# GpSimd's convolution multiplies: one operation of 512 columns in place of two of 256

## Reference

```python
qkvz = x @ W_in                                   # 128 -> q, k, v, z of 1024 each
qkv = conv_general_dilated(concat([q, k, v]), conv_w,      # four taps, one filter per channel,
                           padding=[(3, 0)], ...)          # over the tokens of one sequence
q, k, v = split(silu(qkv))
q = l2norm(q) * HD ** -0.5;  k = l2norm(k)        # 16 heads of 64
def step(S, inp):                                 # per token, per head
    S = S * exp(gt)
    S = S + k (v - k S) * beta
    o = q S
y = norm_w * rmsnorm(o) * silu(z);  x = x + y @ W_o
```

## Time and profile before

| | |
|---|---|
| median of 3 runs | 6077.84 us (6057.86 to 6098.86) |
| the profiled execution | 6087.45 us, of which 6085.7 us from the first to the last instruction |
| PE busy | 5156.0 us (85%) |
| DVE busy | 3611.1 us (59%) |
| ACT busy | 2854.3 us (47%) |
| POOL busy | 2789.0 us (46%), 3045 instructions |
| mean granted TensorE clock | 0.930 |

### The profile page before, as it was taken

One profiled execution on the slowest core, in us unless ns is written; L12 is line 12 of the kernel. 1 busy time (PEld: TensorE's weight loads), 2 busy tenths in 40 slices (PEclk: granted clock), 3 DMA queues, 4 the chain that ended last, 5 costly groups with the idle time before them and its releaser, 6 DMA issues. The chain is left out here.

```text
span 6085.7 us, 206341 instructions
## 1 busy us (share of the span) xinstructions
PE 5156.0 (85%) x78381; PEld 3866.5 (64%) x78382; DVE 3611.1 (59%) x6984; ACT 2854.3 (47%) x5746; POOL 2789.0 (46%) x3045
## 2 busy tenths in 40 slices
PE   4899999999999999999999776688887899994496
PEld 3666666666666666666666555566665666663496
DVE  6666666666666666666666664544444666664443
ACT  1555555555555555555555413333332455451175
POOL 5766666666666666666666533400001000005453
PEclk9999999999999999999999988899898999995598
DMA  3000000000000000000000103200000000001124
GB/s 111 20 25 25 24 25 25 23 24 23 25 25 24 25 24 25 24 25 25 24 25 25 39 20 65 66 1 0 0 0 2 1 0 0 0 0 54 36 70 128
DMA packets 126297, 167.29 MB, mean 27 GB/s; under 512 B 33016, under 2 KB 110880, under 8 KB 123052
## 3 DMA queue, kind: packets, MB, share of 16 engines
q1 hardware_dynamic: 94924, 123.07, 6.7%
q0 software_dynamic: 14080, 26.64, 1.3%
q10 hardware_dynamic: 16640, 8.39, 0.7%
HBM read 118.84 MB, written 105.69 MB: 37 GB/s over the span
## 5 line engine op out<-in xcount | busy, mean ns | idle before, releaser
L934 PE MATMUL bank<-wc,shifted 128*128 128x512 f32 (+1 forms) x2344 | 1055.9, 570 | 19.0 <-issue 15.7
L1324 ACT ACTIVATE TT<-bank 128x512 bf16<-128x512 f32 x640 | 374.0, 595 | 540.7 <-PE bank L1060 289.4
L934 PEld LDWEIGHTS bank<-wc,shifted 128*128 128x128 f32 x2344 | 403.6, 194 | 299.3 <-issue 287.0
L1411 POOL TENSOR_TENSOR qa<-qa,qt 128x512 f32<-128x512 f32 x390 | 487.7, 1272 | 34.8 <-POOL qt L1406 34.8
L1406 POOL TENSOR_TENSOR qt<-qp,cq 128x256 f32<-128x256 f32 x780 | 474.6, 639 | 23.2 <-POOL qa L1411 23.2
L1089 PE MATMUL bank<-X,kqe 64*64 64x64 f32 x12480 | 447.1, 221 | 24.7 <-DVE rb L1593 19.6
L1640 DVE TENSOR_TENSOR yb<-bank,masks 128x512 bf16<-128x512 f32 x512 | 352.0, 687 | 185.6 <-PE bank L1041 185.6
L1089 PEld LDWEIGHTS bank<-X,kqe 64*64 64x64 f32 x12480 | 399.7, 134 | 71.1 <-issue 52.5
L1324 ACT ACTIVATE T<-bank 128x512 bf16<-128x512 f32 x512 | 287.1, 595 | 252.4 <-PE bank L1053 250.4
L3280 DVE TENSOR_REDUCE mxp_full<-bank_full 128x2 f32<-128x512 f32 x524 | 325.7, 685 | 108.7 <-PE bank_full L3029 108.7
L1041 PEld LDWEIGHTS bank<-T,mTb 128*128 128x128 bf16 x5120 | 202.7, 97 | 253.1 <-ACT T L1324 81.1
(11 more groups left out here) (547 smaller groups left out, 12974.1 us busy)
## 6 DMA issues: line engine op xcount, KB each, us to landing
sent_l0f<-blank_l0f SPq DMA_DIRECT2D x64, 528.0 KB
sent_l1m<-blank_l1m SPq DMA_DIRECT2D x64, 528.0 KB
xin<-sent_l1m SPq DMA_DIRECT2D x139, 66.0 KB
taken_l1m<-back_l1m SPq DMA_DIRECT2D x16, 512.0 KB, 8.7
xin<-sent_l0f SPq DMA_DIRECT2D x75, 66.0 KB
x_sb<-in_L_attn_x_dram SPq DMA_DIRECT2D x32, 128.0 KB, 2.9
cw_stage<-in_L_attn_conv_w_dram SPq DMA_DIRECT2D x4, 1024.0 KB, 6.5
x_rows<-x_sb ACTq DMA_DIRECT2D x8, 512.0 KB, 11.8
```

Of the source, the lines that this page charges most:

```text
L934: mm = pe.matmul(bk[:, cols], src[:, j, :], w["wc"][:, j, at * 512 + cols.start:at * 512 + cols.stop], start=(j == 0), stop=(j == TAPS - 1 ...
L1324: nc.scalar.activation(dst, bk[:, :].rearrange("p (h a u) -> p h a u", h=8, u=1 << l), ACT.Copy).then_inc(actb.done.sem, 1)
L1411: ins = pool.tensor_tensor(qa[:, H, :], qa[:, H, :], qt[:, H, :], ALU.add)
```

## The change

In `convolve` the loop over the two sequences goes; one multiply of 4 groups x 2 sequences x 64 columns takes their place. The access pattern of its input steps over groups, over sequences (67 columns apart) and over tokens; the tap is broadcast over the last two. The waits, the adds and all else stay as they are. One convolution has 8 multiplies of 512 columns and the same 6 adds.

```diff
                 for n, j in enumerate((TAPS - 1, *range(TAPS - 1))):
                     for half, H in enumerate(halves):
-                        for s in range(NB):
-                            at = s * (LEAD + BS) + j
-                            tap = w["cq"][:, H, j:j + 1].to_broadcast([P, 4, BS])
-                            ins = pool.tensor_tensor((qt if n else qa)[:, H, of(s)], qp[:, H, at:at + BS], tap, ALU.mult)
+                        x = qp[:, H, :].rearrange("p k (s n) -> p k s n", s=NB)[:, :, :, j:j + BS]
+                        tap = w["cq"][:, H, j:j + 1].unsqueeze(3).to_broadcast([P, 4, NB, BS])
+                        ins = pool.tensor_tensor((qt if n else qa)[:, H, :].rearrange("p k (s n) -> p k s n", s=NB), x, tap,
+                                                 ALU.mult)
                         if n and half:
                             chain(b, ins)
```

## The result

The changed kernel takes 6170.79 us (median of 4 runs, 6151.45 to 6182.0) against 6088.35 (4 runs, 6057.86 to 6098.9): ratio 1.014, 95% interval 1.009 to 1.019. The profiled executions are 6149.7 and 6085.7 us from the first to the last instruction.

The account below looks back on a forecast made before the run. PE's program order was taken to bound the delta stage. DVE's delays of 3.56 us a turn over 16 turns, 57.0 us, less 1.2 once, gave +56 us: 6077.84 to 6134 us, range 6090 to 6170.

Parts of the forecast that it names:

- The price of the operation: POOL's new 512-column multiply in the convolution: 1.05 us at the broadcast rate, 0.43 more than the old one.
- The turn-taking, t = 1, 2, 3: DVE's masks and copy wait for whole POOL multiplies at tile start: +1.14, +0.86 and +0.86 us a tile.
- t = 0: First tile of each loop turn: DVE held 1.28 us longer, less PE's slack, leaving +0.70 us.
- slack 0.58: In t = 0, PE's second level_zero group could have started 0.58 us earlier, absorbing that much of DVE's delay.
- What DVE loses PE loses: At level_zero PE waits for add_out, then continues in program order, so DVE's delay passes to PE: 3.56 us a turn.
- The gain of 1.2 us ahead of the loop: ACT waits for the first convolution, so its shorter POOL time saves 1.2 us once.
- No gain in the loop from POOL's 1.2 us: Each convolution saves 1.2 us of POOL, worth nothing in the loop, since POOL waits for PE's gate chunk anyway.
- no pattern price: Denies the rival that the new multiply has no saving or a pattern price, 1.24 to 1.52 us; chance 0.13.
- no absorption: Denies the rival that a later PE wait shrinks by as much as tile start is delayed, 6077 us; chance 0.15.
- no gain: Denies the rival that POOL is late at the tile's end, up to 1.2 us gained each, 6001 us; chance 0.06.
- the price rival: POOL's new multiply has no saving or costs extra for its pattern: 6168 to 6194 us; chance 0.13.

Follow-up runs that it names:

- x2: Changed kernel with only taps 3 and 0 in 512-column multiplies, taps 1 and 2 back in 256: ratio 1.017 to the kernel before, loop 3322.5 us.
- x1: Changed kernel with only taps 1 and 2 in 512-column multiplies, taps 3 and 0 back in 256: ratio 0.998 to the kernel before, loop 3227.0 us.
- x9: Changed kernel with taps 3 and 0 in multiplies of 128 columns, taps 1 and 2 in 512: ratio 0.992 to the kernel before, loop 3193.6 us.
- x3: Changed kernel, PE makes the first group's level_zero matmuls five times over in t = 1, 2, 3: ratio 1.012 to the kernel before, loop 3292.0 us.
- x5: Changed kernel, POOL starts its convolution only after DVE's add_out of the tile before: ratio 0.993 to the kernel before, loop 3175.9 us.
- x6: Kernel before (256 columns), POOL's convolution waits for DVE's add_out of the tile before: ratio 0.990, loop 3177.7 us.
- x4: Kernel before, PE makes the first group's level_zero matmuls three times over in t = 1, 2, 3: ratio 1.001, loop 3226.5 us.
- x8: Changed kernel, row copy ahead of rsqrt_k, POOL's wait for add_out ahead of the state's multiply too: ratio 0.989 to the kernel before, loop 3176.5 us.

## Why the prediction was wrong

Slower was forecast, and was right; 6134 us was forecast with 6170 as the end of the range, 6170.8 came. A turn was to grow by 3.5 us and grew by 6.1. The changed kernel's own timed runs could not tell this from the forecast (+56 us is the low end of their interval); the loop's 96 us and x2's 1.013 to 1.021 do. Step by step:

- **The price of the operation** (1.05 us, from the broadcast rows): 1.053 measured. The third level of the pattern cost nothing. The Trainium skill, page GPSIMD Engine Reference, section "2.1 Instruction dispatch", has about 2.5 cycles an element as a floor for two inputs. By the estimate from it the operation would have taken about 1.15; the measurement decides against it where one input is broadcast.
- **The turn-taking, t = 1, 2, 3**: mask and copy were forecast at 1.43 and 1.47 us and show 1.43 and 1.47; the tiles were forecast 1.14, 0.86 and 0.86 us longer and are 1.15, 0.9 and 0.86. x1, x2 and x9 show the cause. The trace agrees with what the Trainium skill, page SBUF — State Buffer, section "Who interferes with whom", says of a VectorE instruction with two SBUF inputs beside a GpSimd one that reads SBUF: the masks show 0.69 us alone, and 0.78, 1.00 and 1.43 beside multiplies of 128, 256 and 512 columns.
- **t = 0**: forecast 0.70, measured 1.1. The mechanism was right, the term "slack 0.58" mis-sized. I read it in one turn, in which the loop cost PE 1.33 us of issue. Over the 15 turns it costs 0.9 to 1.4, 1.05 in the mean, so PE mostly comes earlier than in the turn I read. One turn on, in the kernel before:

```profile
1410.33 1.96 PE L934 MATMUL bank<-wc,shifted 128*128 128x512 f32 x4 [0.99 <-issue]
...
1411.86 0.27 DVE L1552 TENSOR_TENSOR x_sb<-x_sb,bank 128x128 f32 x1
1412.12 0.64 PE L1029 MATMUL bank<-identb,mTb 128*128 128x64 bf16 x16
```

  By the same working the second group starts near 1412.44 and could start at 1412.19: slack 0.25, so 1.28 - 0.25 = 1.03. The forecast's 0.7 us of new wait there is 0.9 in the changed kernel. Over the loop this is some 5 us.
- **"What DVE loses PE loses"**: this is the step that failed, because it stops there. PE lost the 63 us of longer holes and another 33 by the half clock, on work that it had ready. The forecast put this term at nothing without a word. The loop's mean granted clock of 0.99 in the earlier trace rows looked like full speed, but it held one slow stretch a turn already, which cost 1.2 us. With the term the loop's growth is 63 + 33 = 96 us. That 6078 + 96 = 6174 comes within 4 us of the median is partly luck, since the median of the kernel before moved from 6078 to 6088 with one more run. x3 shows this term by itself: more work in the hole, less time.
- **The gain of 1.2 us ahead of the loop** didn't show: from the first convolution's start to the second's it is 38.85 us before and 38.68 after.
- **No gain in the loop from POOL's 1.2 us**: right. POOL's wait for PE's gate chunk at L1485 went from 1.0 us a time (63.2 in 63) to 3.7 (225.0 in 61). That is 2.7 us more where 1 to 2 were forecast: 1.2 from the shorter convolution, and 1.5 by which PE's tile is longer. x5 against x6 shows that the width is worth nothing even with POOL started later.
- **The rivals**: no pattern price (1.05 us), no absorption (the tiles grew by what DVE was held), no gain. The upper end of the range was made from the price rival. That the measured time lies beside it has another reason, the clock, and is luck.

## What to carry to other kernels

Before making a GpSimd instruction longer, look at which VectorE instructions run beside it and who waits for them: if the two take turns, each VectorE instruction there pays for the longer one whole, and a few shorter multiplies at the meeting point, or a wait that moves GpSimd past it, are worth more than fewer instructions (loops of 3194 and 3176 us against 3227 and 3323). An engine with slack gains nothing by being faster; here the same wide multiplies cost 1.7% in one place and 0 in another. And a hole on a busy TensorE is to be priced twice, by its length and by the half clock that may follow; a mean granted clock of 0.99 can already hold some of that.

## What the runs showed of the hardware

- VectorE's masked multiply with two SBUF inputs, or its SBUF copy, and a GpSimd multiply held each other off for whole instructions, in strict turns, with GpSimd multiplies of 128, 256 and 512 columns: the copy shows 0.73 us alone, 0.82, 1.04 and 1.47 in turns. `add_out`, which has one input in PSUM, was never held (0.26 to 0.29 us in every tile of the changed kernel).
- Holes of 2.1 to 2.3 us on an otherwise full PE were followed by 3.4 us at 1.2 GHz in 18 of 47 tiles (t = 1, 2, 3), 1.6 us of time each, and again in 18 of 47 in x2; with 1.3 us of repeated matmuls in the hole this happened in none. Holes of 1.2 us in the same place were followed by it in none of 47.
- The number of slow stretches changed from kernel to kernel in places that no edit touched (time at 1.2 GHz of 55, 61, 10, 20 and 61 us in the kernel before, x4, x5, x6 and x8), so a kernel with shorter tiles at full clock can come out the same, as x8 did.
